# A deep-factorization recommender on one core: in each group of product tiles every second tile multiplies its low parts first, then its high parts

## The reference, cut to what matters

```python
inputs = emb[feature_ids] * feature_vals[:, :, None]
h = inputs
for i in range(3):
    x = jnp.einsum('bhd,bmd->bhmd', h, inputs).reshape(B, -1, 16)
    x = jax.nn.relu(jnp.einsum('bcd,oc->bod', x, Ws[i]) + bs[i][None, :, None])
    h, direct = (x[:, :100], x[:, 100:]) if i != 2 else (h, x)
    finals.append(direct)
d = jax.nn.relu(inputs.reshape(B, -1) @ dnn_W0.T + dnn_b0)
d = jax.nn.relu(d @ dnn_W1.T + dnn_b1)
out = (jnp.concatenate((cin_result, d), axis=1) @ fc_W.T + fc_b)[:, 0] + jnp.sum(input_biases, axis=1)
```

## Time and profile before

| | |
|---|---|
| time, median of 3 runs | 2737.98 us (2735.11 to 2738.59) |
| the profiled execution's own time | 2738.99 us |
| its span, first to last instruction | 2737.1 us |
| TensorE busy | 2631.7 us, 96% |
| weight loads busy | 2625.4 us, 96% |
| VectorE, GpSimd, ScalarE busy | 84%, 85%, 67% |

### The profile page before, as it was taken

How to read it: one execution, slowest core, us unless ns; L and a number is a source line. 1 busy time by engine, 2 the same in 40 slices (tenths; PEclk the granted TensorE clock), 3 DMA queues, 4 the chain that set the end, 5 groups by cost and what they waited for, 6 DMA issues and landing times.

```text
span 2737.1 us, 68364 instructions
## 1 busy us (share of the span) xinstructions
PE 2631.7 (96%) x17790; PEld 2625.4 (96%) x17790; DVE 2295.9 (84%) x4619; ACT 1831.6 (67%) x4784; POOL 2321.4 (85%) x2168
## 2 busy tenths in 40 slices
PE   0599999999999999999999999999999999999998
PEld 0599999999999999999999999999999999999998
DVE  3688888888888888888888888888888888888885
ACT  0566776766767767676676767677677766777663
POOL 6799888988889888898889888899889988877763
PEclk9799999999999999999999999999999999999999
DMA  8844544445444454554545445454554545544441
GB/s 153 198 130 129 136 132 134 128 121 137 134 133 133 123 151 120 135 131 122 152 119 137 130 128 146 119 141 125 140 136 121 138 124 142 136 121 138 119 113 54
DMA packets 245794, 359.91 MB, mean 131 GB/s; under 512 B 69023, under 2 KB 163298, under 8 KB 245474
## 3 DMA queue, kind: packets, MB, share of 16 engines
q1 hardware_dynamic: 231538, 352.70, 46.6%
q0 software_dynamic: 10496, 2.88, 2.9%
q10 hardware_dynamic: 3568, 2.71, 0.3%
HBM read 354.19 MB, written 14.17 MB: 135 GB/s over the span
## 4 chain that ended last, share of the span: by engine, by line
PE 93%; SPq 2%; DVE 2%; issue 1%; ACTq 1%; DMA 1%; POOL 0%; ACT 0%; POOLq 0%; DVEq 0%
PE acc L675 60%; PE acc L676 28%; PE acc L700 3%; PE hrep L711 1%; ACTq L827 1%; DVE W L1127 0%; SPq L332 0%; SPq L322 0%; SPq L389 0%; DMA odd<-lin 0%; DMA xrep<-lin_ab 0%; POOL xlo_p L580 0%; PE acc L775 0%; PE acc L776 0%; PE acc L777 0%
## 5 line engine op out<-in xcount | busy, mean ns | idle before, releaser
L675 PE MATMUL acc<-W,xhi_d 128*128 128x400 f32 x5632 | 1729.3, 366 | 16.7 <-DVE xlo_d L1153 7.2
L676 PE MATMUL acc<-W,xlo_d 128*128 128x200 f32 x5632 | 1438.4, 255 | 0.0
L1153 DVE TENSOR_TENSOR xlo_d<-prod_d,xhi_d 128x512 fp32r<-128x512 f32 (+1 forms) x1536 | 984.3, 641 | 192.8 <-ACT xhi_d L860 125.5
L1145 DVE TENSOR_TENSOR prod_d<-hrep,xrep 128x512 f32<-128x512 f32 (+1 forms) x1536 | 1039.1, 677 | 107.3 <-issue 33.4
L675 PEld LDWEIGHTS acc<-W,xhi_d 128*128 128x128 f32 x5632 | 1060.2, 188 | 19.3 <-DVE xlo_d L1153 8.6
L676 PEld LDWEIGHTS acc<-W,xlo_d 128*128 128x128 f32 x5632 | 1078.6, 192 | 0.0
L860 ACT ACTIVATE xhi_d<-prod_d 128x512 fp32r<-128x512 f32 (+1 forms) x1536 | 884.2, 577 | 215.5 <-PE acc L676 204.4
L580 POOL TENSOR_TENSOR xlo_p<-prod_p,xhi_p 128x512 fp32r<-128x512 f32 (+1 forms) x768 | 922.3, 1201 | 121.4 <-ACT xhi_p L854 86.0
L675 PE MATMUL acc<-W,xhi_p 128*128 128x400 f32 x2816 | 880.5, 363 | 14.9 <-POOL xlo_p L580 14.9
L569 POOL TENSOR_TENSOR prod_p<-hrep_s,xrep 128x512 f32<-128x512 f32 x512 | 667.5, 1304 | 111.4 <-ACT hrep_s L897 72.0
L676 PE MATMUL acc<-W,xlo_p 128*128 128x200 f32 x2816 | 719.6, 256 | 0.0
(11 more groups left out here) (110 smaller groups left out, 1206.1 us busy)
## 6 DMA issues: line engine op xcount, KB each, us to landing
xrep<-xs SPq DMA_DIRECT2D x384, 384.0 KB
xrep<-xs SPq DMA_DIRECT2D x384, 128.0 KB
xrep<-xs SPq DMA_DIRECT2D x128, 336.0 KB
l0x<-xs SPq DMA_DIRECT2D x504, 80.0 KB
l0x<-xs SPq DMA_DIRECT2D x252, 63.0 KB
l0x<-xs SPq DMA_DIRECT2D x630, 7.0 KB
xrep<-xs SPq DMA_DIRECT2D x128, 64.0 KB
l0x<-xs SPq DMA_DIRECT2D x126, 64.0 KB
```

The source lines that it names most:

```text
L675: pe.matmul(bank[:, 0:2 * OUTS], hi, w, start=first, stop=last, skip_group_check=True)
L676: return pe.matmul(bank[:, 0:OUTS], lo, w[:, 0:OUTS], start=False, stop=last, skip_group_check=True)
L1145: nc.vector.tensor_tensor(to, h, xrep[:, (par + layer - 1) % 2, a:a + count, :], ALU.mult).then_inc(s_prod_d, 1)
L1153: op = nc.vector.tensor_tensor(xlo_d[:, slot, 0:split], bank[:, 0:split], xhi_d[:, slot, 0:split].bitcast(F32), ALU.subtract)
```

## The change

`split_tile` gets an argument, `turned`, which is true for the second and fourth tile of a group. A turned tile issues the `lo` multiply first (line 677 of the new kernel) and the `hi` one behind it (line 678). The first multiply of a bank, which clears it, is never in a turned tile. Other tiles are as before (now lines 679 and 680). No operand, count or wait changes.

```diff
-            def split_tile(bank, hi, lo, w, first, last):
+            def split_tile(bank, hi, lo, w, first, last, turned):
+
+                if turned:
+                    pe.matmul(bank[:, 0:OUTS], lo, w[:, 0:OUTS], start=False, stop=last, skip_group_check=True)
+                    return pe.matmul(bank[:, 0:2 * OUTS], hi, w, start=False, stop=last, skip_group_check=True)
                 pe.matmul(bank[:, 0:2 * OUTS], hi, w, start=first, stop=last, skip_group_check=True)
                 return pe.matmul(bank[:, 0:OUTS], lo, w[:, 0:OUTS], start=False, stop=last, skip_group_check=True)
...
-                        mm = split_tile(bank, hi, lo, w, start, end)
+                        mm = split_tile(bank, hi, lo, w, start, end, n % 2 == 1)
```

## The result

| | before | changed |
|---|---|---|
| median of 6 runs | 2737.52 us | 2754.62 us |
| lowest to highest | 2735.11 to 2738.59 | 2752.51 to 2756.02 |
| span of the profiled execution | 2737.1 us | 2753.7 us |

The ratio of the changed kernel's time to the one before is 1.0062, with a 95% interval of 1.0052 to 1.0072. The forecast was 2731.0 us in a range of 2724 to 2748; the time lies above the range.

A forecast was written before the change was run, and what follows sets the result against it. The prediction took TensorE's pace through its own queue as the bound; terms 0 + 0 - 10.3 (`hi` behind `hi`) + 3.3 (transposes) = -7.0 us gave a median of 2731.0 us, range 2724 to 2748.

The forecast's parts named there:

- What bounds the kernel: Whole span: the pace at which TensorE, busy 96%, gets through its own queue.
- The rule for a slot: Each multiply in the loop takes the longer of its own time (`hi` about 0.181) and the next load (0.108 us).
- The transposes: Two per step behind a now turned tile: lighter load falls in an H slot, L rises to 0.108; +3.3 us.
- H behind H: A `hi` multiply right behind a `hi`, 3969 places: load already there, 2.6 ns less each, -10.3 us.
- L behind L: A `lo` multiply right behind a `lo`, 4224 turned tiles: no extra cost, taken as 0, bounds 0 to +8.4 us.
- Loads against multiplies: Per two tiles: each H hides a load, each L exposes its end, 0.585 us in both orders; term 0.
- Three loads in a row cost: Rival at each L behind L: 0.0016 us on each, no H behind H gain, +10.1 us, 2748.1; chance 0.13.
- Only the loss is real: Rival: H behind H saves nothing and the 3.3 us at the transposes remain, 2741.3 us; chance 0.31.
- The much faster rival: Exposed load end paid per change from L to H, first L of a pair 0.095; 2676 us, chance 0.06.
- The signs of being wrong: L behind L at 0.12 or more, H behind H longer than H behind L, or TensorE waiting for a group.

The follow-up runs named there:

- two H and two L: Against the kernel before: two tiles at a time, both high multiplies first, then both low ones (H0 H1 L0 L1); 2741.8 us, ratio 1.0018.
- Rotations by one and by three: Kernel before, high and low still alternating, each low multiply that of the tile one or three places on in its group; 2748.9 and 2749.2 us.
- plain at the transposes: Changed kernel, but the last tile of groups P3 and D10, ahead of each transpose, is not turned; 2752.1 us, ratio 1.0050 to the kernel before.
- aligned rows: Every tile's moving operand starts at a multiple of 512 bytes of the weights; 2758.0 us in the order of before, 2745.3 us in the turned order.
- 300 columns in the order of before: Kernel before, with the low multiply over 300 columns instead of 200; 2958.7 us, ratio 1.0797.
- four H and four L: Against the kernel before: each group issues its high multiplies first, all four, then its low ones; 2740.1 us, ratio 1.0005.
- rotation by two: Kernel before, high and low still alternating, each low multiply that of the tile two places on in its group; 2740.7 us, ratio 1.0006.

## Why the prediction was wrong, point by point

**What bounds the kernel: right.** The loss is all in TensorE's queue; its waits in the layers did not grow.

**The rule for a slot: right to some ns.** The slot is the longer of the multiply's own time and the next load: 100 columns instead of 200 leave the L slot where it was, 300 make it 0.138. The 2 to 3 ns in a slot that the rule says nothing of make up nearly the whole loss.

**The transposes: the sum right, the split wrong, and in part luck.** Forecast +3.3 us, with the L at 0.108 and the gap behind the load of line 715 at 0.18. Taking out the turned tiles ahead of the transposes gives 0.027 per step, 3.4 us. But that gap is 0.165 and the one ahead of it 0.136, because the transpose's load starts late, and the 3.4 us are a loss of 6.4 at these places less 3 that other slots gave back.

**H behind H: right in sign and about in size.** Forecast 2.6 ns less than H behind L today (0.1847); the slots are 0.1825, 2.3 ns less, -9.3 us where -10.3 was forecast. It could have been read: over 80 steps the three H behind H of the kernel before have 0.182.

**L behind L: this step failed, by its size.** Taken as 0, with a bound of +8.4 us from a slot of 0.110. It is 0.111, 2.7 ns more than L behind H, +10.7 us and past the bound, which came from three transposes with a lighter load. For H behind H the prediction chose the run of ten slots because it is read ten times more finely; here it chose one single gap of 0.11, which is good to some 5 ns, against three gaps that gave 0.110.

**Loads against multiplies, "Term: 0": this step failed.** It held that an H behind an L costs what it did, whatever comes ahead. It went from 0.1848 to 0.1873, at some 4000 places, +9.8 us. This and the L behind L are 20 of the 24 us between the forecast and the result. The prediction priced pairs of neighbours only by kind and by load. The runs showed in its place that a few ns in each H slot depend on the order in which the moving rows of `W` are read, as long as multiplies wait for loads. Told by the experiments instead of by the slots, the 0.140 us per step are 0.027 for the transposes, 0.033 for the pairs on net, gains of H behind H included (two H and two L against before), and 0.080 for H slots behind an L, which are dearer in the turned order than in the order of two and two.

**The rivals.** "Three loads in a row cost" had the right sign and is a part of it, with 0.13 of the chances; at 10.1 us it was too small, and its 1.6 ns per pair was 2.7. "Only the loss is real" was wrong, since H behind H does gain. The much faster rival is refuted: the first L of a pair has 0.108, not 0.095. The Trainium skill, page "TensorE: Matmul & The Clock Gate", section "Part 2: What happens when you issue a matmul", says that the queue pulls weight loads ahead of multiplies in flight where they go to the background weight buffer. The traces agree for one load; no trace shows more than one ahead.

**The range** ended at 2748 because each unknown was bounded by rows of neighbouring pairs, and an effect of the succession of rows had no row before that named it. It stood in the trace, though: the H slots of the kernel before are not equal but repeat in the patterns given above, of which 0.18 and 0.19 can be seen in the earlier trace rows. I averaged them instead of asking what makes them differ. The signs of being wrong that I had named did not come either: L behind L stayed under 0.12 (but for the two places where the transpose's load starts late), H behind H is the shorter of the H slots, and TensorE waited no longer for a group. None of them asked whether an H behind an L keeps its 0.1847.

**What stays open.** By what rule the step from one moving row to the next costs or saves a few ns, and why an L behind an L has 2.7 ns more. Rotations by one and by three tiles cost 9 to 11 us, by two about 2; a row is 1600 bytes, so odd steps differ from even ones by 64 bytes in their rest by 128. But with every rest equal, the plain order is the slow one, so "equal rests are good" is not the rule either.

One regularity any rule has to meet. The mean step of 18 of the 20 traces is a whole multiple of 6.667 ns, to 0.2 ns: 3012 of them in the kernel before, 3033 in the changed one, 3029 when plain at the transposes, 3017 with two and two, 3026 rotated by one, 3037 and 3021 with aligned rows. In the other two (300 columns in the order of before, and 100) three steps together are. The pattern of four tiles in the kernel before takes 176 of these units, the one of three tiles with aligned rows 133. So the multiplies fall into a repeating pattern that fits such a grid, and a price of some ns per place is a mean over that pattern, not a property of the place. 6.667 ns are 16 cycles at 2.4 GHz, and 64 bytes of a row are 16 columns; whether the two belong together no run shows. Nor is it shown why the effect is gone when no load is waited for.

No version beat the kernel before; the nearest, four H and four L and the rotation by two, were level with it within what the times can tell; their steps are 0.013 and 0.020 us longer.

## What to carry to other kernels

Where a stream of multiplies alternates between hiding its weight loads and waiting for them, an order that looks the same by count can differ by 0.6% through some ns per multiply; measure it, and measure it again if the layout of the moving operand changes, since the sign of the difference may change with it. Read such an effect from the spacing of load starts over tens of loop rounds, which is good to 1 ns, and test it by making the short multiply longer than its load: if the effect vanishes, the wait has a part in it. Do not add up prices per place to a ns either: a change at one place moved the slots at others.

## What the runs showed of the hardware

A weight load of 128 columns for these multiplies takes 0.108 us from start to start at the 2.4 GHz level, and a second one behind it, when neither is hidden, 0.111. Only one load was ever ahead. Each load started behind the start of the multiply ahead of its own, never before it. A low multiply of 232 columns has the same slot as one of 200 or 100, 0.108 (the whole kernel takes 0.2% longer with 232). Transposes load lighter: the slot in which they load can be 0.095. And the slot of a 400-column multiply behind an L that waited for a load varied between 0.185 and 0.188 in the mean, by the rows that the multiplies ahead of it had read; a shift of all buffers by 64 bytes did not move it. The mean step of the loop was a whole multiple of 6.667 ns in 18 of 20 traces.
